# Weights of a DLRM tower kernel: W1 turned first, then W2 and W0, with no W2 left for the loop

## The reference, cut to what matters

```python
e = stack([tbl_j[ids[:, j]] for j in range(39)], axis=1)     # (512, 39, 16), f32
def cin_layer(X0, Xi, W, b):                                 # W: (128, 39 * Fi)
    return einsum('hjk,bjd,bkd->bhd', W.reshape(128, 39, Fi), X0, Xi) + b[None, :, None]
X1 = cin_layer(e, e,  W0, b0)      # Fi = 39
X2 = cin_layer(e, X1, W1, b1)      # Fi = 128
X3 = cin_layer(e, X2, W2, b2)      # Fi = 128
h = concat([X1.sum(2), X2.sum(2), X3.sum(2), dense_ctx], axis=1)      # (512, 400)
y = relu(relu(h @ W_top1 + b_top1) @ W_top2 + b_top2) @ W_top3        # (512, 1)
```

## Time and profile before

| | us |
|---|---|
| median of 3 runs | 691.94 (691.92 to 692.39) |
| the profiled execution | 694.63 |
| its span in the trace | 692.5 |

### The profile page before, as it was taken

One profiled execution on the slowest core, in us unless ns is written; L12 is line 12 of the kernel. 1 busy time (PEld: TensorE's weight loads), 2 busy tenths in 40 slices (PEclk: granted clock), 3 DMA queues, 4 the chain that ended last, 5 costly groups with the idle time before them and its releaser, 6 DMA issues.

```text
span 692.5 us, 11925 instructions
## 1 busy us (share of the span) xinstructions
PE 658.8 (95%) x2662; PEld 475.0 (69%) x2662; DVE 593.3 (86%) x958; ACT 560.8 (81%) x1941; POOL 358.8 (52%) x394
## 2 busy tenths in 40 slices
PE   2788999999999999999999999999999999999898
PEld 2655777776767777677767676777667777767584
DVE  2557898999999998999999998999899999999870
ACT  2546889989888987988888887898799888899762
POOL 7734783746566464648383746557463415132700
PEclk9999999999999999999999999999999999999999
DMA  8216622314040504141322314050414140200000
GB/s 281 23 17 116 161 38 55 67 32 90 14 105 8 112 8 109 13 104 17 95 27 63 57 38 80 16 103 8 109 12 107 11 101 7 64 19 1 1 1 0
DMA packets 67394, 39.65 MB, mean 57 GB/s; under 512 B 58646, under 2 KB 61718, under 8 KB 65204
## 3 DMA queue, kind: packets, MB, share of 16 engines
q1 hardware_dynamic: 60463, 37.71, 24.4%
q0 software_dynamic: 5120, 1.29, 2.2%
q10 hardware_dynamic: 1760, 0.15, 0.2%
HBM read 32.80 MB, written 2.40 MB: 51 GB/s over the span
## 4 chain that ended last, share of the span: by engine, by line
PE 77%; DVE 6%; ACT 6%; issue 6%; DMA 3%; ACTq 0%; SPq 0%; POOL 0%; DVEq 0%; POOLq 0%
PE yb L979 18%; PE yb L980 17%; PE yb L981 17%; PE p L945 13%; ACT yb L624 5%; PE pq L956 4%; DVE acc L803 4%; DMA gram<-in_L_rec_W_dram 2%; PE pq L910 1%; PE yb L1085 1%; PE yb L897 1%; DMA late<-x_scratch 1%; DVE yb L789 1%; PE p L1057 1%; PE p L1055 1%
## 5 line engine op out<-in xcount | busy, mean ns | idle before, releaser
L624 ACT ACTIVATE yb<-yb,x0t 128x128 f32<-128x128 f32 x1728 | 468.9, 383 | 78.4 <-PE yb L981 71.6
L803 DVE TENSOR_TENSOR acc<-acc,yb 128x512 f32<-128x512 f32 (+1 forms) x576 | 385.3, 669 | 40.6 <-ACT yb L624 9.3
L979 PE MATMUL yb<-w1h,x1h 128*128 128x512 f32 (+1 forms) x640 | 315.3, 493 | 8.4 <-DVE acc L803 5.7
L980 PE MATMUL yb<-w1l,x1h 128*128 128x512 f32 (+1 forms) x640 | 248.1, 388 | 0.0
L981 PE MATMUL yb<-w1h,x1l 128*128 128x512 f32 (+1 forms) x640 | 248.1, 388 | 0.0
L979 PEld LDWEIGHTS yb<-w1h,x1h 128*128 128x128 f32 x640 | 120.3, 188 | 90.0 <-DVE acc L803 60.0
L476 POOL TENSOR_TENSOR late<-late,x0r 117x512 f32<-117x512 f32 (+1 forms) x105 | 132.0, 1290 | 88.7 <-DMA late<-x_scratch 88.5
L422 POOL DMA_INDIRECT emb<-in_table_dram,idx x160 | 152.6, 954 | 43.0 <-issue 38.8
L980 PEld LDWEIGHTS yb<-w1l,x1h 128*128 128x128 f32 x640 | 121.0, 189 | 41.2 <-issue 24.9
L981 PEld LDWEIGHTS yb<-w1h,x1l 128*128 128x128 f32 x640 | 120.4, 188 | 24.8
L465 POOL TENSOR_TENSOR bdiag<-mask,x0t 128x312 f32<-128x312 f32 x64 | 45.4, 710 | 156.3 <-PE pq L956 153.0
(11 more groups left out here) (108 smaller groups left out, 317.1 us busy)
## 6 DMA issues: line engine op xcount, KB each, us to landing
late<-x_scratch SPq DMA_DIRECT2D x45, 312.0 KB
late<-x_scratch SPq DMA_DIRECT2D x30, 234.0 KB
emb<-in_table_dram,idx POOLq DMA_INDIRECT x160
gram<-in_L_rec_W_dram SPq DMA_DIRECT2D x1, 2496.0 KB, 12.2
x_scratch<-x0r SPq DMA_DIRECT2D x15, 156.0 KB
late<-x_scratch SPq DMA_DIRECT2D x15, 156.0 KB
w2t<-in_L_rec_W_dram SPq DMA_DIRECT2D x1, 1280.0 KB, 15.6
x0t<-embt SPq DMA_DIRECT2D x64, 20.0 KB
```

The costliest lines, as they stand in the source:

```text
L624: op = act.activation(part, part, ACT.Copy, scale=x0t[u][:, t, j:j + 1])
L803: dve.tensor_tensor(part, part, parts(y_bank(t, m), n), ALU.add).then_inc(summed, 1)
L979: pe.matmul(y[:, 0:w], hi, w1h[:, at:at + w], start=True, stop=False)
L980: pe.matmul(y[:, 0:w], hi, w1l[:, at:at + w], start=False, stop=False)
```

## The change

W1 is loaded first, in three pieces (banks 0 to 2, 3 to 5, 6 to 9), then W0, then all of W2 in two pieces. `TURN_ORDER` lists the 22 banks: W1's ten, four of W2, the two of W0, the other six of W2. ACT copies W1, W0 and six banks of W2 (`W2_BY_ACT`), DVE the other four. DVE makes all of W1's low parts before it folds W0. `dims_outside(0)` and ACT's `samples` stand behind the last copy of W0. The five slots of W2 in the loop, their waits and the later load are gone. The gathers of group 1 wait for the last ten of ACT's 18 copies; those of group 2 wait, one each, for the seven products of group 0 and for ACT's first three scaled banks.

```diff
+W1_CUTS = (0, 3, 6, 10)
+W2_CUTS = (0, 5, 10)
+W2_FIRST = 4
+W2_BY_ACT = (0, 1, 2, 3, 6, 8)
...
+        TURN_ORDER = ([("W1", b) for b in range(W_BANKS)] + [("W2", b) for b in range(W2_FIRST)] +
+                      [("W0", b) for b in range(W0_BANKS)] + [("W2", b) for b in range(W2_FIRST, W_BANKS)])
...
         def _(sp):
             sp.dma_start(base[:, :], bases).then_inc(ids_in, 16)
             sp.dma_start(ids_all[:, :, :], ids).then_inc(ids_in, 16)
+            for h in range(len(W1_CUTS) - 1):
+                w = columns_of(W1_CUTS[h], W1_CUTS[h + 1])
+                sp.dma_start(w1raw[:, w], W1[:, w]).then_inc(w1_in[h], 16)
             sp.dma_start(w0raw, W0).then_inc(w0_in, 16)
-            sp.dma_start(w1raw, W1).then_inc(w1_in, 16)
-            w = w2_columns(W2_PIECES[0], W2_PIECES[1])
-            sp.dma_start(w2flat[:, w], W2[:, w]).then_inc(w2_in[0], 16)
+            for h in range(len(W2_CUTS) - 1):
+                w = columns_of(W2_CUTS[h], W2_CUTS[h + 1])
+                sp.dma_start(w2flat[:, w], W2[:, w]).then_inc(w2_in[h], 16)
...
                     if u == 1:
-                        pool.wait_ge(w_hi, W0_BANKS + W_BANKS - PER_Q + i + 1)
+                        pool.wait_ge(w_hi, act_copies(TURNS - 1) - PER_Q + i + 1)
                     gather(u, i)
...
             for i in range(PER_Q):
+                if i < CHUNKS:
+                    pool.wait_ge(pairs_ready, i + 1)
+                else:
+                    pool.wait_ge(act_scaled, i - CHUNKS + 1)
                 gather(0, i)
...
-            for n in range(W0_BANKS):
-                copy_weights(n)
-            for n in range(W0_BANKS, W0_BANKS + W_BANKS):
-                if n == DIMS_TURN:
+            for n in range(TURNS):
+                if by_act(n):
+                    copy_weights(n)
+                if TURN_ORDER[n] == ("W0", W0_BANKS - 1):
                     dims_outside(0, 0, 0)
                     act.wait_ge(embq_ready, 1)
                     samples(act, 0, 0, range(QUARTERS // 2, QUARTERS))
-                copy_weights(n)
...
+            for n in range(W_BANKS):
+                low_weights(n)
             dve.wait_ge(w0_in, 16)
...
-                        if isinstance(g, int) and (T, m) in W2_SLOTS:
-                            turn_w2(T, m, W2_FIRST + W2_SLOTS.index((T, m)))
```

More of the change, by code:

```diff
@@ L83 @@
 WARM = 24
-DIMS_TURN = 7
 EARLY = 4
@@ L194, in tower @@
         w0_in = sem("w0_in")
[L195 to L198, removed]
+        w1_in = [sem(f"w1_in{h}") for h in range(len(W1_CUTS) - 1)]
+        w2_in = [sem(f"w2_in{h}") for h in range(len(W2_CUTS) - 1)]
         shifted_ready = sem("shifted_ready")
@@ L272, in tower, with by_act, by_dve, act_copies @@
         W0_BANKS = -(-CHUNKS // 4)
-        TURNS = W0_BANKS + W_BANKS + W2_FIRST
-        def w2_columns(b0, b1):
+        TURN_ORDER = ([("W1", b) for b in range(W_BANKS)] + [("W2", b) for b in range(W2_FIRST)] +
+                      [("W0", b) for b in range(W0_BANKS)] + [("W2", b) for b in range(W2_FIRST, W_BANKS)])
+        TURNS = len(TURN_ORDER)
+        W0_AT = TURN_ORDER.index(("W0", 0))
+        def by_act(n):
+            kind, b = TURN_ORDER[n]
+            return kind != "W2" or b in W2_BY_ACT
+        def by_dve(n):
+            return TURN_ORDER[n][0] == "W1" or not by_act(n)
+        def act_copies(n):
+            return sum(by_act(k) for k in range(n + 1))
+        def dve_copies(n):
+            return sum(by_dve(k) for k in range(n + 1))
+        def columns_of(b0, b1):
             return slice(4 * b0 * HID, min(4 * b1, FIELDS) * HID)
[L279 to L285, removed]
         def split_weights(b):
@@ L550, in copy_weights @@
             def copy_weights(n):
+                kind, b = TURN_ORDER[n]
                 act.wait_ge(w_turned, n + 1)
-                if n < W0_BANKS:
-                    for i in range(4 * n, min(4 * n + 4, CHUNKS)):
+                if kind == "W0":
+                    for i in range(4 * b, min(4 * b + 4, CHUNKS)):
                         rows = ROWS if i < CHUNKS - 1 else LAST_ROWS
@@ L832, in period @@
                                               ALU.subtract).then_inc(ctx_low, 1)
-            for n in range(W0_BANKS, TURNS):
-                low_weights(n)
+            for n in range(W_BANKS, TURNS):
+                if by_dve(n):
+                    low_weights(n)
             dve.wait_ge(x0r_ready, 1)
@@ L893, in turn_weights @@
                 else:
[L894 to L897, removed]
+                    raw, landed, cuts = (w1raw, w1_in, W1_CUTS) if kind == "W1" else (w2flat, w2_in, W2_CUTS)
+                    if b in cuts:
+                        pe.wait_ge(landed[cuts.index(b)], 16)
+                    for j in range(4 * b, min(4 * b + 4, FIELDS)):
+                        op = pe.transpose(yb[n % RING][:, (j - 4 * b) * HID:(j - 4 * b + 1) * HID],
                                           raw[:, j * HID:(j + 1) * HID], ident[:, :])
@@ L924, in turn_shifted @@
                 op.then_inc(shifted_turned, 1)
[L926 to L935, removed]
             def layer0(g, c):
@@ L1023, in _ @@
                     turn_shifted(c + 2)
[L1024 to L1025 removed]
+            pe.wait_ge(w_hi, act_copies(TURNS - 1))
+            pe.wait_ge(w_lo, dve_copies(TURNS - 1))
             period(0, 0, 2)
```

74 lines of the change are left out of this document (25 added, 49 removed).

## The result

| us | before | after |
|---|---|---|
| median of 11 runs each | 691.94 (690.01 to 693.86) | 696.07 (693.52 to 697.98) |
| the profiled execution, its span | 694.63, 692.5 | 695.98, 693.9 |

The ratio is 1.0058, 95% interval 1.0043 to 1.0073: slower by 4.1 us. The forecast was 693.9 in a range of 690.4 to 695.9, so the sign was right and the size was half; 696.07 lies outside.

The account below looks back on a forecast made before the run. PE's work was taken to hold 77% of the way to the end, after a head that hangs on `embq`. Terms +3.8 (`embq`), +0.3 (chain) and -2.1 (loop) gave +2.0 on the median 691.94: 693.9, range 690.4 to 695.9.

Parts of the forecast that it names:

- Steps 1 to 4: Head: W1, W0's fold, four W2 banks at half pace, then W0 delay `embq` from 19.52 to 23.3, +3.8 us.
- the sum: Whole kernel: the head's +3.8 and +0.3 and the loop's -2.1 make +2.0 us.
- Step 5: Head: W2's other six banks are turned during the two rounds of transfers and cost nothing.
- Step 6: Group 0, `x0a` to layer 1: PE waits longer and starts at half pace, +0.3 us (-0.8 to +1.7).
- Step 7: Loop: W2's 19 transposes leave a full PE, -2.1 us (-2.4 to -1.2).
- Step 8: Gathers of groups 1 and 2: their new waits cost nothing, bounds 0 and +0.5 us.
- B: Rival: PE keeps its clock or W2 lands at 16.6, so head loses what loop gains; +0.1, 692.0, chance 0.24.
- C: Rival: the two rounds of transfers before `x0a` get shorter; -1.6, 690.3, chance 0.18.
- D: Rival: W1 lands at 14.4, fold ends late, clock stays low through group 0's chain; +4.5, 696.4, chance 0.10.
- A: The forecast itself: `embq` held back by W0 behind W2 at half pace; +2.0, 692.3 to 695.5, chance 0.48.

Follow-up runs that it names:

- e2: The changed kernel with `dims_outside(0)` and `samples` behind W2's second bank instead of behind W0: 693.88 us, ratio 1.0003 to the kernel before.
- e4: The changed kernel with W0 loaded, folded and turned first again, then W1, then all of W2 ahead of the loop: 695.43 us, ratio 1.0035 to before.
- e1: The kernel before, unchanged, run for a second profile: 694.34 us, ratio 1.0009.
- e3: The changed kernel with 68 idle transposes on PE in place of 24: 693.34 us, ratio 0.9992 to the kernel before.
- e13: The kernel before with only the ten waits of group 2's gathers added, on a chip where before takes 714.51: 698.86 us, ratio 0.9784.
- e16: The changed kernel, unchanged, on the chip where the kernel before takes 714.51: 701.48 us, ratio 0.9814 to before.
- e6: The kernel before with W2's second half loaded at the start, on a chip where before takes 714.59: 713.84 us, ratio 0.9989.
- e14: The kernel before with W2's second half loaded at the start, on a chip where before takes 714.51: 714.86 us, ratio 1.0007.
- e17: The kernel before with only the ten waits of group 2's gathers added, on a chip where before takes 714.98: 699.14 us, ratio 0.978.

## Why the prediction was wrong

**Steps 1 to 4, `embq` at 23.3 (+3.8):** right in place, 0.8 too high (+2.99). The fold ended at 19.41 (forecast 20.0), W2's first turn came at 17.43 (17.4) at half pace (PEclk 0.51 in 18 to 20), and `embq` at 22.51. The sentence ahead of it, that only its place on ACT holds `embq`, was wrong: e2 and e4 show that the gathers land at about 22 when all of W2 stands in the queue. Both gates open within 0.4 us of each other (22.16 in e2, 22.51), so the number came out near by luck, while one of its two reasons was missing.

The rule of the Trainium skill ("TensorE: Matmul & The Clock Gate", Part 1), that an idle TensorE goes back to the slow clock, was weighed for W2's banks, where the trace agrees (idle 4.29, then PEclk 0.51). The same rule bore more on the idle time before group 0's chain, 5.77 us, and there the sum gave it 0.3. From the Trainium skill, "DMA: Bandwidth & Descriptors", "Queues, rings and completion order", the prediction took that other queues get their turn between packets. W1's and W2's landings fit it; the gathers, on another queue, landed only when the weights had (19.1 against 22.2), so in these runs their turns did not get them through sooner.

**Step 5, W2's other six banks: nothing.** Right: PE turned them by 24.3, and `x0a` came at 31.37.

**Step 6, `x0a` to layer 1 (+0.3, bounds -0.8 to +1.7): this is the step that failed.** Measured 18.24 against 16.04, +2.2 in the two profiles, and +3.9 against what the kernel before can do, 14.36 in e1. The step saw that the idle time would grow and priced it from an execution that had itself lost the clock there, as if that were the rule. It also bounded the growth at +1.7, from a clock that comes back 1.7 later; PEclk was 0.50 until 42. e3 fills the idle time and has 14.36 again, and with 3.0 us of the 3.9 kept to group 2's mark the loss is gone (ratio 0.9992). (The 1.71 that the step read as layer 0's first matmul is two matmuls in the earlier trace rows.)

**Step 7, the loop (-2.1): right.** 2.34 between the marks of groups 2 to 4, the 2.3 us of PE's work that left.

**Step 8, the gathers: nothing.** Group 1's last was issued at 28.98 (28.85 before). No wait of 1 us or more on group 2's is in the profile after. On chips of the other kind the pacing alone, put into the kernel before, gained more than the whole change (e13 against e16), which no row of before could show.

**The sum against the profile.** The two profiled spans differ by 1.4 us, near the +2.0 of the sum, and partly by luck: the head lost 5.3 where the sum had 4.1, and 0.7 between layer 1 and the first mark and 0.8 behind the third came back, which no term contains. The medians differ by 4.1. The prediction took the 2.7 us by which the profiled execution stood above the median as common to both kernels, and this is where the failed step reaches the forecast. It wasn't common: after's profile was at its own median (695.98, 696.07). The executions of the changed kernel lose more of the clock than those of the kernel before. The mean granted clock of a whole execution shows it: 0.983 to 0.990 in the changed kernel's eleven, 0.990 to 0.998 in the 35 of the kernel before beside e1, 0.988 to 0.998 in e3. The means, 0.987 and 0.995, lie 0.008 apart, which over 694 us is at most 5.5 us of TensorE's work (an estimate, and an upper one, since PE also idles in slow stretches). Of the 2.7 us e1 shows 1.7 in the chain, of which 1.1 is left at group 2's mark; for the rest no row was found. One profile says little at this size: e1 and e3 lie 1.39 apart at group 4's mark (146.68, 148.07) and 0.2 the other way in their spans.

**The rivals.** B and C are out: B needed W2's banks at full clock or W2 in at 16.6, and they were turned from 17.43 at PEclk 0.51; C's shorter rounds did not come, 8.86 against 8.77. D, at 696.4, came nearest, half by luck: of its two causes W1's late landing did not come (14.4; PE turned it by 13.1), while the low clock through group 0's chain did, at +2.2 where D had +1.0. The chances do not add up as written: a third of A's 0.48 taken away, A and D leave 0.42 for slower, not 0.48.

## What to carry to other kernels

Price a longer idle time on TensorE from the length of the work behind it at full clock (14.36 us here, 18.24 after 5.77 us of idle time), and not from one execution that may already have paid. A clock that is kept in one stretch may fall in the next, so read what it is worth some way further on (3.0 of 3.9 us here). When a step is held by its place in an engine's list, ask what would hold it next: here the gathers' landing stood right behind, and moved with the bytes that were queued up front. A profile is one execution on one chip: the same two kernels stood at 1.006 in the result and at 0.984 and 0.981 on two other chips.

## What was not expected of the hardware

On four of the chips instructions started 2 to 15 us late in the first 50 us of the program, with a releaser "remote" that no profile of the result or of e1 to e4 has in that stretch. ("issue" alone shows nothing: the 5.77 us of the kernel after, ahead of group 0's chain, are a wait for `x0a`.) The longest, 15.00 and 15.18 us on ACT (e6, e14), have their input ready 13 us before they start. They fall together with POOL's unpaced gathers, and with these paced they are gone from the profiles (e13, e17), with ratios of 0.978 on two chips. Waits of 2 to 4 us are left there. That the instruction itself had not arrived is one reading, since the profile names no engine as the releaser, but it is argued and not shown: the profile's two instruction queues have no packet in the middle of that wait (34 to 46 us in e6). Why these chips do so and those of the result and of e1 to e4 do not stays open.
